# A sigmoid recurrence on one core: the sum in PSUM started by VectorE and finished by TensorE, instead of a product that VectorE adds to

## The chip, the core and the metric

The kernel runs on one core of one Trainium2 chip. The metric is the device time of one execution in microseconds (us); lower is better. TensorE does the matrix products, VectorE and ScalarE the elementwise work on its results in PSUM (eight banks of 512 fp32 columns by 128 partitions), GpSimd works in SBUF only, and SyncE issues most transfers. All data are fp32.

## The reference

A convolutional block with attention and two spectral mixers comes first, and its output is `x` plus a correction. The change lies behind it, in a recurrent layer:

```
Wx = einsum('bti,hi->bth', ln(t), W)   # t: x as 4 batches of 4096 tokens of 128 values
Wx = (Wx - mean) * rsqrt(var + eps) * gamma + beta   # mean and var over all tokens
def step(y, wx_t):
    y = sigmoid(wx_t + y @ V.T)
    return y, y
y0 = 0
_, ys = scan(step, y0, Wx over T)
out = t + ys
```

## The kernel before

The layer's input has 4 batches (`NB`) of 4,096 tokens; each batch is one chain of 4,096 steps of a state with 128 features. The recurrence forgets its start quickly, so the kernel cuts every chain into chunks of `STEPS` = 16 steps and runs all chunks side by side. Every chunk first does `BURN` = 8 steps on the tokens of its own second half from a guessed state, and what that yields is handed to the following chunk as its start; then come the 16 real steps. That makes 24 rounds. A round handles all 1,024 chunks, as four groups `g` = 0..3 (`GR`), one per batch, each a block of 128 features by 256 chunks (`Q` = 8 by `TB` = 32).

In a round a group passes three engines, in one fixed order of instructions on each, and semaphores hand it on:

1. TensorE multiplies the group's last state `y_s` by V into PSUM bank `g` (even rounds of a pair) or `g + 4` (odd ones), 128 x 256 columns: `sums(g, dj)`. It waits for semaphore `state`. Every fp32 product appears in the trace as two weight loads and two MATMUL records. In `from_last`, once in the program (at the first real step, step 0), the state comes from the neighbouring chunk, so it is three products: 1 column of zeros, 31 columns and 224 columns.
2. VectorE adds the scaled input (`add_z`, line 1570): bank = wx_step * bs + bank. It waits for `vy` and signals `vy_wx`.
3. ScalarE takes the sigmoid of the bank into `y_s` (lines 1146 and 1155, unrolled copies of one statement, 256 columns) and signals `state`. In round 0 it needs no product: it reads the scaled input from SBUF with the bias `bb_guess` (line 1142).

So there are 23 rounds with products: seven of four 256-column products, one with `from_last`, and fifteen more of four 256-column products. The body of the loop at the end of `recur` (`e.If(again > 0)`) runs only if the guess was not good enough, which does not happen with these inputs.

Just ahead of the recurrence, 32 products W x are written to SBUF with sums for the normalization (VectorE line 1546, ScalarE line 1133), then a short chain on VectorE (lines 1555 to 1565) makes the scale `bs` and the biases `bb` and `bb_guess`. TensorE there does one product of 1 column for the row sums of V (`v_sum_filled`) and `WARM` = 4 products of 512 columns whose result nobody reads. Behind the recurrence, TensorE transposes the states back (line 636, four transposes for each of 32 results), VectorE adds them to the residual (line 1613), and SyncE stores each result with a transfer of 256 KB. VectorE's check of the guess (lines 1594 to 1604) and the engines' read of the flag come behind that. GpSimd adds `g0` to the residual in 32 pieces (line 620), 21 of them during the recurrence, and then copies the handed-on starts (`start_kept`, line 626), which ScalarE waits for ahead of the last round.

Further ahead, where the second mixer's factors are made, VectorE copies `bet` (line 1513), `z0t` (line 1514) and `g0` (line 1517) out of bank 3; GpSimd waits for `bet`.

The names of lines 632 (products) and 636 (transposes) are those of helpers, `mm` and `tr`; line 400 is the helper `copy`.

Of the kernel before, what the change touches and what calls it, by code (L numbers as in the profile page):

```python
# [67 lines left out]
G0_EARLY, WARM = 11, 4  # L68
# [6 lines left out]
GR = NB  # L75
TOL = 1e-5
# [75 lines left out]
def metaformer(nc, t, out):  # L152
# [4 lines left out]
    with ctx:  # L157
# [289 lines left out]
        def unrolled(n, turn):  # L447

            for i in range(1, n):
                turn(i)  # L450

        def recur(e, sweep, results=None, judge=None):


            def looped(n, turn):
                with e.Fori(1, n) as i:
                    turn(i)


            sweep(0, STEPS - BURN, unrolled)  # L460
            sweep(BURN, 0, unrolled)
            rounds = BURN + STEPS
            if results:
                results(0)
            if judge:
                judge(rounds)
            e.wait_ge(S("judged"), 1)
            again = e.value_load(FLAG[0:1, 0:1], min_val=0, max_val=1)
            with e.If(again > 0):
# [4 lines left out]
                with e.Fori(0, CHUNKS - 1) as i:  # L474
                    sweep(i * STEPS + rounds, 0, looped)
                e.wait_ge(S("state"), GR * (rounds + STEPS * (CHUNKS - 1)))
                if results:
                    results(2)
            e.wait_ge(S("state"), GR * rounds)
# [150 lines left out]
        def _(pe):  # L630
# [228 lines left out]
            def skip_factors(n):  # L859


                if n == 4:
                    pe.wait_ge(S("dg2"), 1)
                    mm(PS[:, 3, 128:256], ones, dg)
# [63 lines left out]
            def sweep(k0, j0, turns):  # L928

                for dj in range(0 if j0 == 0 else 1, 2):  # L930
                    for g in range(GR):
                        pe.wait_ge(S("state"), GR * (k0 + dj - 1) + g + 1)
                        (mm(sums(g, dj), v_t, at(y_s, g, j0)) if dj else from_last(g)).then_inc(S("vy"), 1)

                def turn(i):
                    for dj in range(2):
                        for g in range(GR):
                            pe.wait_ge(S("state"), i * (2 * GR) + (GR * (k0 + dj) + g + 1 - GR))
                            mm(sums(g, dj), v_t, at(y_s, g, i * 2 + (j0 + dj - 1))).then_inc(S("vy"), 1)

                turns((STEPS - j0) // 2, turn)
# [16 lines left out]
            recur(pe, sweep, results, judge)  # L958
# [3 lines left out]
        def _(act):  # L962
# [175 lines left out]
            def sweep(k0, j0, turns):  # L1138
                for dj in range(2):
                    for g in range(GR):  # L1140
                        if j0 and dj == 0:
# [501 lines left out]
```

## Time and profile before

| | |
|---|---|
| time, median of 3 | 427.39 us (427.3 to 428.25) |
| profiled execution | span 424.2 us from first to last instruction; the results list no time of its own for it, so it is set against the median: 3.2 us lie around the span |
| busy share of the span | TensorE 82%, VectorE 80%, ScalarE 54%, GpSimd 50% |
| recurrence | from 346.6 us (first sigmoid) to 390.3 us (first transpose behind it) |
| results and stores | 390.3 us to about 421 us |

The busy shares are averages over stages that have different limits; the recurrence is about a tenth of the span. A MATMUL record is longer than the distance to the next one, since products are pipelined, and VectorE's and ScalarE's instructions overlap by some 0.1 us as well. So what counts is the distance between starts.

### The profile page before, as it was taken

Reading aid. Unit: us, or ns where it says so; the run is one execution under the profiler, and the core shown is the slowest. Engines: PE = TensorE matmul, PEld = TensorE weight load, DVE = VectorE, ACT = ScalarE, POOL = GpSimd, SP = SyncE. Lnnn points to the kernel's source line nnn. Section 1 sums busy time; section 2 is a strip of 40 time slices with the busy share of each in tenths; the row PEclk is TensorE's granted clock in tenths of the full one; section 3 lists DMA queues with packets and bytes.
Section 4 is the critical chain, followed back from the end, with each engine's and each line's share of the span. In section 5 each row is a group of like instructions: output and inputs, shape, how many; then the busy total and the mean of one; then the engine's idle time right before and its main releaser. Section 6 shows DMA issues by size and latency. Waiting matters only on the chain.

```text
span 424.2 us, 7190 instructions
## 1 busy us (share of the span) xinstructions
PE 349.7 (82%) x2415; PEld 273.7 (65%) x2415; DVE 338.0 (80%) x995; ACT 229.5 (54%) x511; POOL 213.0 (50%) x261
## 2 busy tenths in 40 slices
PE   0289979997794899998999778878888789999950
PEld 0289965974352899987988748634454446767950
DVE  2999762766896967469999686999999759899991
ACT  0498851801023388545655125767886789899000
POOL 1389960000002699399892107887886579900000
PEclk9999999999998699999999969899999999999995
DMA  8999998999805000089799880142232500000998
GB/s 215 249 291 319 288 284 191 220 218 379 339 0 199 2 0 2 2 100 116 91 174 119 100 99 2 46 156 100 101 103 107 192 2 0 2 0 0 276 287 234
DMA packets 62999, 59.42 MB, mean 140 GB/s; under 512 B 5792, under 2 KB 55376, under 8 KB 60912
## 3 DMA queue, kind: packets, MB, share of 16 engines
q1 hardware_dynamic: 43232, 50.24, 40.0%
q0 software_dynamic: 16512, 8.39, 16.2%
q10 hardware_dynamic: 3216, 0.30, 0.7%
q8 instruction: 21, 0.34, 0.3%
q14 instruction: 18, 0.15, 0.1%
HBM read 38.84 MB, written 16.94 MB: 131 GB/s over the span
## 4 chain that ended last, share of the span: by engine, by line
DVE 34%; PE 32%; POOL 12%; DMA 6%; issue 5%; SPq 4%; ACT 4%; DVEq 0%; POOLq 0%; ACTq 0%
PE PS L632 30%; POOL BIG L569 8%; DVE SML L1196 6%; DVE BIG L1337 5%; DVE BIG L1529 4%; DVE BIG L1546 3%; SPq L511 3%; DMA BIG<-in_x 3%; DVE BIG L1613 3%; POOL BIG L588 2%; DMA BIG<-BIG 2%; PE PS L636 2%; DMA BIG<-xn_rows 2%; DVE BIG L1429 1%; DVE BIG L1425 1%
## 5 line engine op out<-in xcount | busy, mean ns | idle before, releaser
L632 PE MATMUL PS<-CST,BIG 128*128 128x128 f32 (+6 forms) x994 | 123.0, 312 | 13.1 <-ACT BIG L1004 4.5
L632 PEld LDWEIGHTS PS<-CST,BIG 128*128 128x128 f32 (+1 forms) x994 | 110.2, 193 | 28.8 <-DVE BIG L1529 8.3
L582 POOL COPY BIG<-BIG 128x512 f32<-128x512 f32 x24 | 29.9, 1291 | 79.2 <-DMA BIG<-xn_rows 75.3
L632 PE MATMUL PS<-BIG 128*128 128x128 f32 (+2 forms) x450 | 53.8, 368 | 5.9 <-DVE BIG L1337 5.4
L1196 DVE BATCH_NORM_STATS2 SML<-BIG 128x6 f32<-128x128 f32 x256 | 53.5, 279 | 5.8 <-DMA BIG<-in_x 4.4
L636 PEld LDWEIGHTS PS<-CST,BIG 128*128 128x128 f32 (+1 forms) x326 | 41.6, 183 | 19.5 <-issue 12.4
L632 PEld LDWEIGHTS PS<-BIG 128*128 128x128 f32 (+2 forms) x450 | 40.6, 168 | 16.7 <-issue 8.7
L636 PE MATMUL PS<-CST,BIG 128*128 128x128 f32 (+1 forms) x326 | 49.0, 291 | 2.5 <-ACT SML L400 1.4
L632 PE MATMUL PS<-BIG,SML 128*128 128x256 f32 (+4 forms) x230 | 48.8, 415 | 0.0
L400 ACT ACTIVATE BIG<-PS 128x512 f32<-128x512 f32 (+3 forms) x59 | 32.2, 569 | 26.0 <-PE PS L632 21.0
L569 POOL TENSOR_SCALAR BIG<-BIG,SML 128x128 f32<-128x128 f32 x84 | 40.3, 498 | 9.0 <-DVE SML L1216 9.0
L1570 DVE SCALAR_TENSOR_TENSOR PS<-BIG,SML,PS 128x256 f32<-128x256 f32 x92 | 41.2, 488 | 3.3 <-PE PS L632 3.2
L588 POOL TENSOR_TENSOR BIG<-BIG,SML 128x512 f32<-128x512 f32 x32 | 39.6, 2495 | 7.3 <-ACT BIG L1078 7.3
L632 PE MATMUL PS<-SML 128*128 128x512 f32 (+2 forms) x74 | 35.2, 560 | 9.4 <-DVE BIG L1546 8.0
L611 POOL TENSOR_TENSOR BIG<-BIG 128x512 f32<-128x512 f32 x32 | 40.8, 1275 | 0.5 <-ACT BIG L1104 0.5
L632 PEld LDWEIGHTS PS<-BIG,SML 128*128 128x128 f32 (+1 forms) x230 | 31.0, 178 | 15.2 <-ACT BIG L1155 3.4
L620 POOL TENSOR_TENSOR BIG<-BIG,SML 128x512 f32<-128x512 f32 x32 | 32.0, 1041 | 9.2 <-issue 6.3
L1155 ACT ACTIVATE BIG<-PS,SML 128x256 f32<-128x256 f32 x80 | 35.5, 475 | 0.4
L632 PE MATMUL PS<-SML,BIG 128*128 128x128 f32 (+1 forms) x264 | 33.2, 287 | 1.4 <-DVE SML L1383 1.0
L632 PEld LDWEIGHTS PS<-SML,BIG 128*128 128x128 f32 (+1 forms) x264 | 32.2, 203 | 2.5 <-DVE SML L1383 1.3
L1088 ACT ACTIVATE BIG<-BIG,SML 128x512 f32<-128x512 f32 x32 | 22.8, 720 | 19.0 <-DVE BIG L1425 19.0
L604 POOL TENSOR_TENSOR BIG<-BIG,SML 128x256 f32<-128x256 f32 x32 | 19.6, 613 | 24.4 <-DVE SML L1513 12.5
(218 smaller groups left out, 487.3 us busy)
## 6 DMA issues: line engine op xcount, KB each, us to landing
xn_rows<-BIG SPq DMA_DIRECT2D x8, 1024.0 KB, 9.4
BIG<-xn_rows SPq DMA_DIRECT2D x8, 1024.0 KB, 9.2
BIG<-in_x POOLq DMA_DIRECT2D x8, 1024.0 KB, 11.0
BIG<-rs_rows SPq DMA_DIRECT2D x8, 1024.0 KB, 4.7
out_x<-BIG SPq DMA_DIRECT2D x32, 256.0 KB, 3.6
BIG<-wy_rows SPq DMA_DIRECT2D x16, 192.0 KB, 5.8
BIG<-BIG SPq DMA_DIRECT2D x16, 192.0 KB, 8.0
BIG<-in_L_conv_mixer_w SPq DMA_DIRECT2D x2, 544.0 KB, 9.1
```

What stands on the lines that cost most here:

```text
L400: return e.activation(o, i, ACT.Copy) if e is scalar_engine else e.tensor_copy(o, i)
L569: last = pool.tensor_scalar(x_h[:, n, :], x_h[:, n, :], ln_r[:, n:n + 1], ln_b[:, n:n + 1], ALU.mult, ALU.add)
L582: pool.tensor_copy(x_mix[:, g % MIX_RING], columns(g)).then_inc(S("x_mix_pool"), 1)
L588: pool.tensor_tensor(m1[:, v, :], a0[:, v, :], kap[:, v].unsqueeze(2).to_broadcast([128, 4, W]), ALU.mult).then_inc(S("ka0"), 1)
L611: pool.tensor_tensor(a0[:, v, :], a0[:, v, :], m1[:, v, :], ALU.add).then_inc(S("xm"), 1)
L620: pool.tensor_tensor(a0[:, v, :], a0[:, v, :], g0[:, v].unsqueeze(2).to_broadcast([128, 4, W]), ALU.add).then_inc(S("x1_g0"), 1)
L632: return pe.matmul(o, l, rhs, start=start, stop=stop, **k)
L636: return pe.matmul(o, i, ident[0:n, 0:n], is_transpose=True, start=True, stop=True)
L1088: act.activation(v, v, ACT.Gelu, bias=s("cu")).then_inc(S("m1"), 1)
L1155: act.activation(at(y_s, g, i * 2 + (j0 + dj)), sums(g, dj), ACT.Sigmoid, bias=s("bb")).then_inc(S("state"), 1)
L1196: last = dve.bn_stats(ln_st[:, c % 2, row, :], src[:, XR * c + row, :])
L1570: STT(sums(b, dj), wx_step[:, b, :, bass.ds(j, 1), :], s("bs"), sums(b, dj), ALU.mult, ALU.add).then_inc(S("vy_wx"), 1)
```

## The change

- VectorE no longer adds. Ahead of the product it writes `wx_step * bs` into the bank (`seeded(g, r)`, TENSOR_SCALAR from SBUF to PSUM), up to two rounds ahead, as soon as the sigmoid of round r - 2 has read that bank (semaphore `state`).
- TensorE's product then accumulates on it (`accumulate`, start = False) and waits for both `seed` and `state`; it signals `sum`, for which ScalarE waits directly.
- The product of 1 zero column of `from_last` is gone from the unrolled rounds.
- So that accumulation is defined, eight products of 256 columns write to all eight banks first (semaphore `written`). They take the place of the four of 512 columns and wait for `wx` (VectorE's line 1546) instead of `bn` (ScalarE's line 1133).
- The 1-column product for the row sums of V moves from behind `bn` far ahead, next to the product for `bet`, and VectorE copies its column to SBUF there.
- The loop that isn't run keeps the old way.

```diff
-            pe.wait_ge(S("bn"), G4)
-            mm(PS[:, 7, 511:512], v_t, ones[:, 0:1]).then_inc(S("v_sum_filled"), 1)
-
-            for k in range(WARM):
-                mm(bank(5), v_t, CST[:, 0:512])
+            pe.wait_ge(S("wx"), G4)
+            for k in range(2 * GR):
+                mm(PS[:, k, 0:N_G], v_t, CST[:, 0:N_G]).then_inc(S("written"), 1)
+
+            def accumulate(g, r):
+
+                o, j = seeded(g, r), step_of(r)
+                if j:
+                    return mm(o.rearrange("d (q j t) -> d q j t", q=Q, t=TB), v_t, at(y_s, g, j - 1), False, True,
+                              skip_group_check=True)
+                a, b = TB * g, TB * g + TB
+                last = y_s[:, :, STEPS - 1, a:b]
+                mm(o[:, 1:TB], v_t, last[:, Q - 1, 0:TB - 1], False, True, skip_group_check=True)
+                return mm(o[:, TB:N_G], v_t, last[:, 0:Q - 1, :], False, True, skip_group_check=True)
+
+            def rounds():
+                for r in range(1, ROUNDS):
+                    for g in range(GR):
+                        pe.wait_ge(S("seed"), GR * (r - 1) + g + 1)
+                        pe.wait_ge(S("state"), GR * (r - 1) + g + 1)
+                        accumulate(g, r).then_inc(S("sum"), 1)
```

```diff
+            def rounds():
+                j = step_of(0)
+                for g in range(GR):
+                    act.activation(at(y_s, g, j), wx_step[:, g, :, j:j + 1, :], ACT.Sigmoid,
+                                   scale=s("bs"), bias=s("bb_guess")).then_inc(S("state"), 1)
+                for r in range(1, ROUNDS):
+                    if r == ROUNDS - 1:
+                        act.wait_ge(S("start_kept"), 2 * GR)
+                    for g in range(GR):
+                        act.wait_ge(S("sum"), GR * (r - 1) + g + 1)
+                        act.activation(at(y_s, g, step_of(r)),
+                                       seeded(g, r).rearrange("d (q j t) -> d q j t", q=Q, t=TB),
+                                       ACT.Sigmoid, bias=s("bb")).then_inc(S("state"), 1)
```

```diff
             dve.tensor_copy(bet, PS[:, 3, 128:256]).then_inc(S("bet"), 1)
+            dve.tensor_copy(s("v_sum"), PS[:, 3, 0:1])
             dve.tensor_copy(z0t, PS[0:64, 3, 256:384]).then_inc(S("z0t"), 1)
...
+            def rounds():
+
+                for r in range(1, ROUNDS):
                     for g in range(GR):
-                        dve.wait_ge(S("vy"), GR * (k0 + dj - 1) + g + 1)
-                        add_z(g, dj, j0 + dj)
+                        if r >= 3:
+                            dve.wait_ge(S("state"), GR * (r - 2) + g + 1)
+                        else:
+                            dve.wait_ge(S("written"), GR * (r % 2) + g + 1)
+                        TS(seeded(g, r).rearrange("d (q t) -> d q t", t=TB), wx_step[:, g, :, step_of(r), :],
+                           s("bs"), None, ALU.mult).then_inc(S("seed"), 1)
```

On TensorE, from the last three products W x to the last product of the recurrence, the kernel before has these instructions, with the semaphores that each waits for:

```order
469 L632 MATMUL PS<-SML 128x512 [waits x1,lnw] x3
470 L632 MATMUL PS<-CST,SML 128x1 [waits bn]
471 L632 MATMUL PS<-CST,SML 128x512 x4
472 L632 MATMUL PS<-BIG,SML 128x256 [waits state] x28
473 L632 MATMUL PS<-SML 128x1 [waits state]
474 L632 MATMUL PS<-BIG,SML 128x31
475 L632 MATMUL PS<-BIG,SML 128x224
476 L632 MATMUL PS<-SML 128x1 [waits state]
```

and the changed kernel these:

```order
470 L630 MATMUL PS<-SML 128x512 [waits x1,lnw] x3
471 L630 MATMUL PS<-CST,SML 128x256 [waits wx]
472 L630 MATMUL PS<-CST,SML 128x256 x7
473 L630 MATMUL PS<-BIG,SML 128x256 [waits state,seed] x28
474 L630 MATMUL PS<-BIG,SML 128x31 [waits state,seed]
475 L630 MATMUL PS<-BIG,SML 128x224
476 L630 MATMUL PS<-BIG,SML 128x31 [waits state,seed]
```

The unread products have changed their size and what they wait for, the 1-column products are gone, and each product of the recurrence waits for two semaphores.

On VectorE the end of the normalization's chain and the recurrence read like this before:

```order
531 L1563 TENSOR_TENSOR SML<-SML 128x1 [waits dve_seq]
532 L1565 SCALAR_TENSOR_TENSOR SML<-PS,SML 128x1 [waits v_sum_filled,dve_seq]
533 L1570 SCALAR_TENSOR_TENSOR PS<-BIG,SML,PS 128x256 [waits vy,bn_ab]
534 L1570 SCALAR_TENSOR_TENSOR PS<-BIG,SML,PS 128x256 [waits vy] x91
535 L1613 TENSOR_TENSOR BIG<-BIG,PS 128x512 [waits x1_g0,yt_filled] x32
```

and now:

```order
532 L1581 TENSOR_TENSOR SML<-SML 128x1 [waits dve_seq]
533 L1582 SCALAR_TENSOR_TENSOR SML<-SML 128x1 [waits dve_seq]
534 L1598 TENSOR_SCALAR PS<-BIG,SML 128x256 [waits written,bn_ab]
535 L1598 TENSOR_SCALAR PS<-BIG,SML 128x256 [waits written] x7
536 L1598 TENSOR_SCALAR PS<-BIG,SML 128x256 [waits state] x84
537 L1638 TENSOR_TENSOR BIG<-BIG,PS 128x512 [waits x1_g0,yt_filled] x32
```

The 92 additions that waited for TensorE have become 92 writes that wait for ScalarE of two rounds before.

On VectorE, at the copies out of bank 3, before and then now:

```order
347 L1513 COPY SML<-PS 128x128 [waits z0t_filled]
348 L1514 COPY SML<-PS 64x128
349 L400 COPY BIG<-PS 64x128x4 [waits zt2_filled]
350 L1517 COPY SML<-PS 128x128 [waits g0_filled]
351 L400 COPY BIG<-PS 128x512 [waits ta2_filled]
```

```order
347 L1530 COPY SML<-PS 128x128 [waits z0t_filled]
348 L1531 COPY SML<-PS 128x1
349 L1532 COPY SML<-PS 64x128
350 L402 COPY BIG<-PS 64x128x4 [waits zt2_filled]
351 L1535 COPY SML<-PS 128x128 [waits g0_filled]
```

One copy of a single column stands between those of `bet` and `z0t`.

## Rows read from the trace of the kernel before

**Rows 1.** Chain that ended last, from 330 us: start, length, engine, line.

```profile
343.85 46.63 PE PS L632 x210
```

**Rows 2.** Timeline behind the recurrence: start, length, engine, line, instructions merged.

```profile
390.32 18.82 PE L636 MATMUL PS<-CST,BIG 128*128 128x128 f32 x128
...
391.88 29.17 SPq L538 DMA_DIRECT2D out_x<-BIG  x32
```

**Rows 3.** Timeline of one group's way through a round, 384.4 to 386.4 us.

```profile
384.42 1.60 PEld L632 LDWEIGHTS PS<-BIG,SML 128*128 128x128 f32 x8 [0.19 <-ACT BIG L1155]
...
385.15 0.49 DVE L1570 SCALAR_TENSOR_TENSOR PS<-BIG,SML,PS 128x256 f32<-128x256 f32 x1
...
385.68 0.47 ACT L1155 ACTIVATE BIG<-PS,SML 128x256 f32<-128x256 f32 x1
...
386.20 1.60 PEld L632 LDWEIGHTS PS<-BIG,SML 128*128 128x128 f32 x8 [0.19 <-ACT BIG L1155]
```

**Rows 4.** Timeline at the start of the recurrence, engines PE, PEld, DVE, ACT.

```profile
342.19 0.69 DVE L1546 SCALAR_TENSOR_TENSOR BIG<-PS,BIG 128x512 f32<-128x512 f32 x1 [0.23 <-PE PS L632]
343.85 3.92 PE L632 MATMUL PS<-CST,SML 128*128 128x1 f32 x10 [1.70 <-ACT BIG L1133]
345.32 1.28 ACT L1142 ACT_TABLE_LOAD   x1
346.37 0.16 DVE L1565 SCALAR_TENSOR_TENSOR SML<-PS,SML 128x1 f32<-128x1 f32 x1 [0.29 <-DVE SML L1563]
346.62 2.07 ACT L1142 ACTIVATE BIG<-BIG,SML 128x256 f32<-128x256 f32 x4
347.27 0.19 PEld L632 LDWEIGHTS PS<-BIG,SML 128*128 128x128 f32 x1 [0.33 <-ACT BIG L1142]
347.61 1.49 PEld L632 LDWEIGHTS PS<-BIG,SML 128*128 128x128 f32 x7 [0.16 <-issue]
348.32 1.70 DVE L1570 SCALAR_TENSOR_TENSOR PS<-BIG,SML,PS 128x256 f32<-128x256 f32 x4 [1.79 <-PE PS L632]
348.84 1.26 ACT L1146 ACTIVATE BIG<-PS,SML 128x256 f32<-128x256 f32 x3 [0.15 <-DVE PS L1570]
349.37 0.19 PEld L632 LDWEIGHTS PS<-BIG,SML 128*128 128x128 f32 x1 [0.27 <-ACT BIG L1146]
```

**Rows 5.** Timeline of the weight loads in the round with `from_last`.

```profile
360.10 0.30 PEld L632 LDWEIGHTS PS<-SML 128*128 128x128 f32 x2 [0.20 <-ACT BIG L1155]
...
361.67 0.38 PEld L632 LDWEIGHTS PS<-SML 128*128 128x128 f32 x2
361.97 0.53 PEld L632 LDWEIGHTS PS<-BIG,SML 128*128 128x128 f32 x4
362.49 0.38 PEld L632 LDWEIGHTS PS<-SML 128*128 128x128 f32 x2
```

**Rows 6.** VectorE's groups by shape: count, busy, mean ns of one, idle before.

```profile
L1411 DVE TENSOR_SCALAR BIG<-BIG 128x512 f32<-128x512 f32 x1 | 1.2, 1187 | 0.0
...
L1504 DVE TENSOR_SCALAR BIG<-BIG 128x512 f32<-128x512 f32 x1 | 0.4, 428 | 0.0
```

**Rows 7.** Timeline of GpSimd during the recurrence.

```profile
347.36 20.99 POOL L620 TENSOR_TENSOR BIG<-BIG,SML 128x512 f32<-128x512 f32 x21 [2.92 <-ACT BIG L1142]
```

**Rows 8.** Chain (first two rows) and timeline around the copies out of bank 3.

```profile
256.28 0.20 DVE SML L1513
...
257.27 0.28 DVE SML L1517
...
254.96 0.27 PE L636 MATMUL PS<-CST,BIG 128*64 128x128 f32 x1 [0.39 <-DVE BIG L400]
```

**Rows 9.** Busy time by stretch: PE, PEld, DVE, ACT, POOL, clock, DMA share, GB/s.

```profile
265.20:268.60 3.40, 2.22 (x21) 2.06 (x22) 3.33 (x9) 2.79 (x10) 3.08 (x3) 1.00 0.00 0
268.60:272.00 3.40, 3.40 (x18) 2.67 (x15) 3.26 (x15) 2.97 (x11) 1.80 (x2) 0.51 0.00 0
...
340.50:343.90 3.40, 1.70 (x5) 0.35 (x3) 2.24 (x10) 3.29 (x9) 3.40 (x4) 1.00 0.02 5
```

More of the change, by code:

```diff
@@ L67 @@
 STEPS, BURN = 16, 8
[L68 removed]
+G0_EARLY = 11
 BM_ACT, LEAD, WARM_2 = 2, 6, 3
@@ L75 @@
 GR = NB
+N_G = Q * TB
+ROUNDS = BURN + STEPS
 TOL = 1e-5
@@ L445, in sums, with step_of, seeded, recur @@
             return PS[:, g + GR * dj, 0:Q * TB].rearrange("d (q j t) -> d q j t", q=Q, t=TB)
[L447 to L462, printed above, removed]
+        def step_of(r):
+            return STEPS - BURN + r if r < BURN else r - BURN
+        def seeded(g, r):
+            return PS[:, g + GR * (r % 2), 0:N_G]
+        def recur(e, rounds, sweep, results=None, judge=None):
+            rounds()
             if results:
@@ L465, in recur @@
             if judge:
-                judge(rounds)
+                judge(ROUNDS)
             e.wait_ge(S("judged"), 1)
@@ L926, in from_last, with sweep @@
                 return mm(PS[:, g, TB:Q * TB], v_t, last[:, 0:Q - 1, :])
[L928 to L930 removed]
+            def sweep(k0):
+                for dj in range(2):
                     for g in range(GR):
[L932 to L935 removed]
+                        pe.wait_ge(S("state"), k0 * GR + (GR * (ROUNDS + dj - 1) + g + 1))
+                        (mm(sums(g, dj), v_t, at(y_s, g, 0)) if dj else from_last(g)).then_inc(S("vy"), 1)
+                with pe.Fori(1, STEPS // 2) as i:
                     for dj in range(2):
                         for g in range(GR):
[L938 to L941 removed]
+                            pe.wait_ge(S("state"), i * (2 * GR) + (k0 * GR + (GR * (ROUNDS + dj - 1) + g + 1)))
+                            mm(sums(g, dj), v_t, at(y_s, g, i * 2 + (dj - 1))).then_inc(S("vy"), 1)
             def results(turn):
@@ L956, in judge @@
                 tr(PS[0:1, 0, 0:128], s("gap")).then_inc(S("gap_filled"), 1)
-            recur(pe, sweep, results, judge)
+            recur(pe, rounds, sweep, results, judge)
         @block.scalar
@@ L1149, in turn @@
-                def turn(i):
+                        act.wait_ge(S("vy_wx"), k0 * GR + (GR * dj + g + 1))
+                        act.activation(at(y_s, g, dj), sums(g, dj), ACT.Sigmoid,
+                                       bias=s("bb")).then_inc(S("state"), 1)
+                with act.Fori(1, STEPS // 2) as i:
                     for dj in range(2):
-                        if dj and j0 == 0 and type(i) is int and 2 * i + dj == STEPS - 1:
-                            act.wait_ge(S("start_kept"), 2 * GR)
@@ L1160, in _ @@
-            recur(act, sweep)
+            recur(act, rounds, sweep)
         @block.vector
@@ L1613, in results @@
                     TT(v, v, bank(g % 8), ALU.subtract if turn == 1 else ALU.add).then_inc(S("result"), 1)
-            recur(dve, sweep, results, judge)
+            recur(dve, rounds, sweep, results, judge)
 _NAMES = ["x", "L0_conv_key_w", "L0_conv_key_skip_w", "L0_conv_query_w", "L0_conv_query_skip_w",
```

38 lines of the change are left out of this document (16 added, 22 removed).

## The prediction

> **What bounds the kernel now.** I read the chain that ended last first. Before the stores it runs on TensorE's products without a break from 343.85 us for 46.63 us, through the unread products and the whole recurrence [rows 1]. Behind the recurrence the first transpose starts at 390.32 us, and the stores run from 391.88 us for 29.17 us, all but a few us of what is left of the span [rows 2]. They are issued in a row and start when the first result is there, so what the recurrence gives or takes moves the end by as much.
>
> But "the chain is on TensorE" does not say that TensorE is full. The timeline of one group shows it. Its first weight load begins at 384.42, VectorE's addition at 385.15, ScalarE's sigmoid at 385.68 for 0.47 us, and the load for its next product at 386.20, which had waited for that sigmoid [rows 3]. So a round takes as long as one group's way round: 0.73 (product until addition) + 0.53 (addition until sigmoid) + 0.47 (sigmoid) + 0.05 (until load) = 1.78 us. From 349.37 [rows 4] to 360.10 [rows 5] lie six rounds, which gives it more finely: 10.73 / 6 = 1.788 us. When TensorE never waits, its loads follow each other every (1.49 - 0.19) / 6 = 0.216 us (the row of seven) [rows 4], two to a product of 256 columns: 0.432 us, or 1.73 us for four groups. So the ring of three engines is limited by its latency, yet only 0.06 us a round above TensorE's own rate. That is why removing a stage of 0.53 us from it cannot bring much.
>
> **The recurrence before, taken apart.** The first product streams at 347.61, when the last unread product is through; its load had started at 347.27 [rows 4]. A product streams somewhat behind a load that had waited; I reckon with 0.05 us, an estimate that shifts before and after alike except at the first product. Round 1 lasts until 349.37 + 0.05 = 349.42, that is 1.81. Six rounds of 1.788 make 10.73 and end at 360.15. Fifteen rounds of 1.788 make 26.82 and end at 390.32 [rows 2]; so 363.50 - 360.15 = 3.35 is left for the round with `from_last`, of which one group takes 362.49 - 361.67 = 0.82 [rows 5].
>
> **The change, step by step.**
>
> Addition out of the ring. A group's way round becomes 0.73 + 0.47 + 0.05 = 1.25 us, if ScalarE sees the sum as soon as VectorE did. That is below TensorE's 1.73, so TensorE becomes full and a round costs 1.73. ScalarE can follow: its sigmoids come every (1.26 - 0.47) / 2 = 0.395 us when they are ready [rows 4], against 0.432. So 21 rounds gain 0.060 each: 1.26 us.
>
> VectorE's write. No row shows a TENSOR_SCALAR of 256 columns from SBUF to PSUM. Below stands a TENSOR_SCALAR of 512 columns at 428 ns, above it another of 512 at 1,187 ns [rows 6]; halved for 256 columns these give 0.21 and 0.59 us. The nearest row is the addition that it replaces, with the same SBUF operand, the same scalar and the same output, and one operand more: 0.49 us long, (1.70 - 0.49) / 3 = 0.40 us from start to start [rows 4]. I take 0.40 as the most. It must stay below 0.432 to be hidden. The write for round r needs only the sigmoid of round r - 2, a whole round earlier than the product, so its latency is covered; only its rate could show.
>
> The round with `from_last`. Every small product here costs TensorE a pair of loads that are 0.11 us apart: four loads (31 and 224 columns) begin within 0.53 - 0.19 = 0.34 us [rows 5]. Without the 1-column pair a group takes 0.82 - 0.22 = 0.60, at worst 0.82 - 0.14 = 0.68, if only the streaming of the two shrinks. The round then lasts 2.41 (2.74), and the gain is 3.35 - 2.41 = 0.94 (0.61). I take 0.94, since loads set the pace there.
>
> The start. The eight unread products wait for VectorE's last W x (ends 342.88) instead of ScalarE's last sum (343.85) [rows 4], take 8 x 0.432 = 3.46 us and end at 346.3. So the first product streams at 347.27 + 0.05 = 347.32 instead of 347.61. Its bank is seeded in time: VectorE's chain ends at 346.53 [rows 4], and a write of 0.49 or even 0.59 us is done by 347.15. The four sigmoids of round 0 are done at 346.62 + 2.07 = 348.69 [rows 4], so the fourth group's product is loaded at 348.74, streams at 348.79, and round 2 begins 0.43 later, at 349.22, 0.20 earlier than 349.42. The normalization's chain itself may end 0.2 us earlier, since line 1565 no longer waits for PSUM's column, but that gives nothing: the sigmoid of round 0 starts at 346.62 behind a table load that ends at 346.60 [rows 4].
>
> The moved 1-column product and its copy. On TensorE the product (0.22 us) stands ahead of a stretch in which TensorE idles for 0.39 us waiting for VectorE's copies [rows 8], which hides it; without that cover it would cost 0.22. The copy of one column comes behind `bet`, so GpSimd isn't delayed, but it stands in the chain ahead of `z0t`, `g0` and the first rows of the second mixer. A copy of 128 columns takes 0.20 in that chain [rows 8]; one of a single column takes less. I charge 0.10 (bounds 0 and 0.20).
>
> GpSimd and the end. GpSimd's 21 additions end at 368.35 [rows 7], and ScalarE needs the copies behind them only in the last round, at about 387: they stay hidden. Behind the recurrence nothing changes but that VectorE is free earlier, which the first result doesn't need, as it waits for transposes.
>
> Sum: 1.26 + 0.94 + 0.20 - 0.10 = 2.30 us; by positions, the first transpose starts at 349.22 + 6 x 1.73 + 2.41 + 15 x 1.73 = 388.0 instead of 390.3, and 0.1 later for the copy. The sum is made against the span of 424.2 us, which lies 3.2 below the median; a span of 421.9 and a time of 427.39 - 2.30 = **425.1 us** follow.
>
> **The rivals.**
>
> *The rounds stay as long as they are* (0.18). Only the round with `from_last` and the start gain: 0.94 + 0.20 - 0.10 = 1.04, 426.3 us. For it: the margin is only 0.015 us a product, and each product now waits for two semaphores instead of one, or accumulation onto a bank could stream slightly slower than 0.216. Against it: in a full stretch the load is made one product ahead, so what it waits for may end up to 0.216 - 0.05 = 0.16 us late without harm (with my estimate of 0.05).
>
> *The wait for two semaphores is exposed* (0.05). If it held up each product by 0.05 us, the time from sigmoid to load in rows 3, a product would cost 0.48 and a round 1.93: 21 x 0.14 = 2.9 more, less 1.04: 429.3 us. It decides from 0.015 + 1.04 / 92 = 0.026 us a product on.
>
> *VectorE sets the pace; slower* (0.07). If a write takes as long as the dear row of rows 6 has it, 0.59 us for 256 columns, a round costs 2.37, and the recurrence grows by 21 x 0.58 = 12 us to about 438 us. It decides from about 0.46 us a write on. For it: that row, and that its source is strided like `wx_step`. Against it: the addition with the same strides already manages 0.40.
>
> *GpSimd is slowed so much that ScalarE's last round waits* (within the last case's 0.07, at 0.01). A TENSOR_SCALAR at 428 ns for 512 columns runs faster per column than the addition, so it may use a path into SBUF that GpSimd shares. GpSimd's adds would have to take 1.7 times as long before anything waits (347.36 plus 21 of them plus the copies by 387); at twice they would cost about 5 us, 430 us. By the Trainium skill ("VectorE: DVE Perf Modes", Why PSUM operands drop a tier and Two Vector instructions with no wait between them) a two-port mode reads through an interface shared with GpSimd, but fp32 with a PSUM operand does not get that mode; no run shows it yet.
>
> *TensorE's clock falls in the recurrence* (0.01). The trace has a stretch at the lower level, 1.2 GHz, from 268.6 to 272.0 us, after one in which TensorE was busy for 2.22 of 3.40 us [rows 9]. The change leaves TensorE idle from 346.3 to 347.3. But it idled for 1.70 us before 343.85, and the clock stayed at 2.4 GHz [rows 4, 9]. One such stretch would cost 1.7 us, 426.8 us. The Trainium skill ("TensorE: Matmul & The Clock Gate", What's actually happening) has the clock fall after an idle phase; by that rule the gap here, shorter than the one before, is no danger, and the trace agrees.
>
> *More than forecast* (0.04): products on seeded banks stream faster, or the sum is seen earlier; 424 us or less.
>
> **How the numbers follow.** The forecast has 0.65, with a range of its own from 424.5 to 425.9: the bounds of `from_last` (+0.33), of the copy (-0.10 to +0.10) and of the pace (0.435 instead of 0.432 a product, from the rounding of the row: +0.26), and 0.3 for the scatter of the measurement. The range for 8 in 10 adds the first rival, 424.2 to 426.6. A difference of 0.3% is 1.3 us, about the least that a measurement of this kernel can tell; the line is at 426.1. Faster: 0.65 + 0.04 and a little of the first rival, 0.71. Same: 0.17. Slower: 0.12.
>
> **What would show it.** Right: in the recurrence loads every 0.216 us without waits for ScalarE; rounds of 1.73; sigmoids waiting for TensorE and idle for some 0.05 each; about 2.4 us in the round with `from_last`; VectorE's writes 0.40 or less apart with idle time; the first product at 347.3 + 0.1. Wrong: rounds of 1.79 with waits for `seed`; VectorE without idle time; a first store that isn't 2.3 us earlier; a shift ahead of 340 us of more than 0.2, which I have charged only with the copy and which a different timing of the second mixer's start could bring.

## The result, and the profile after

| | before | after |
|---|---|---|
| median beside each other, 22 runs each | 428.06 us | 426.51 us |
| ratio, with its 95% interval | | 0.9946 (0.9921 to 0.9970) |
| on the 427.39 us of the start | 427.39 us | 425.1 us |
| again, 18 and 12 runs | 427.54 us | 424.67 us, ratio 0.9934 (0.9908 to 0.9960) |
| profiled span | 424.2 us | 420.3 us |
| first sigmoid to first transpose | 43.70 us | 41.39 us |

The changed kernel is faster by 0.5%, 2.3 us (0.9946 is taken over the executions whose clock wasn't held lower than the others', so it isn't the quotient of the two medians; one of the changed kernel's 22 took 611 us at a mean granted clock of 0.56). The two profiles differ by more, 3.9 us, and the table's last line says how much of it belongs to the change: 2.31 us. The rest was there when the first sigmoid began, 1.30 us earlier than in [rows 4], and already at VectorE's copy of `bet`, ahead of which nothing changed but one short product (254.52 us against 256.20, 1.68 earlier); a control run below deals with it.

The chain that ended last, from 330 us to the end (start, length, what), answers to [rows 1]:

```profile
333.89 4.80 DMA BIG<-rs_rows
...
341.61 0.90 ACT BIG L1145 x3
...
344.03 1.28 ACT L1153
345.32 0.61 ACT BIG L1153
346.07 40.81 PE PS L630 x192
386.88 1.16 PE PS L634 x8
```

It now reaches TensorE's products at 346.07, by way of the normalization's chain, the table load of ScalarE and its first sigmoid (both line 1153), and no longer through the unread products. From there to the transposes it is TensorE alone.

The timeline of the tail answers to [rows 2]:

```profile
386.72 18.72 PE L634 MATMUL PS<-CST,BIG 128*128 128x128 f32 x128
...
388.18 29.12 SPq L536 DMA_DIRECT2D out_x<-BIG  x32
```

The transposes start 3.60 us earlier than in [rows 2], the stores 3.70, and the stores take as long as before. So what was gained until 386.7 arrived at the end.

The timeline of all engines in the middle of the recurrence, 380.4 to 382.6 us, answers to [rows 3]:

```profile
380.01 2.63 ACT L1160 ACTIVATE BIG<-PS,SML 128x256 f32<-128x256 f32 x6
380.02 2.75 PE L630 MATMUL PS<-BIG,SML 128*128 128x256 f32 x12
380.08 2.65 DVE L1598 TENSOR_SCALAR PS<-BIG,SML 128x256 f32<-128x256 f32 x6
380.24 2.35 PEld L630 LDWEIGHTS PS<-BIG,SML 128*128 128x128 f32 x11
```

In [rows 3] the loads came in eights, with a wait for ScalarE of 0.19 us between two rows. Here eleven stand in one row without a wait, (2.35 - 0.19) / 10 = 0.216 us apart, the rate of a TensorE that never waits. The sigmoids and the writes run at that pace as well: (2.63 - 0.47) / 5 = 0.432 us.

The start, all engines but GpSimd, answers to [rows 4]:

```profile
341.37 3.72 PE L630 MATMUL PS<-CST,SML 128*128 128x256 f32 x16 [0.83 <-DVE BIG L1564]
...
344.03 1.28 ACT L1153 ACT_TABLE_LOAD   x1
...
344.82 0.16 DVE L1582 SCALAR_TENSOR_TENSOR SML<-SML 128x1 f32<-128x1 f32 x1
345.01 3.20 DVE L1598 TENSOR_SCALAR PS<-BIG,SML 128x256 f32<-128x256 f32 x8
345.32 2.08 ACT L1153 ACTIVATE BIG<-BIG,SML 128x256 f32<-128x256 f32 x4
346.03 0.30 PEld L630 LDWEIGHTS PS<-BIG,SML 128*128 128x128 f32 x2 [1.35 <-DVE PS L1598]
```

The unread products are over at 345.1, the first write starts at 345.01, and the first sigmoid at 345.32 behind the table load that ends at 345.31. The first product is loaded at 346.03, 0.71 us after the first sigmoid starts. The label "<-DVE" is the inference from the last semaphore: the first write, 0.49 us long, had ended at 345.50, and what the load waited for was the first sigmoid (about 0.6 us long, 345.92). Eight writes in 3.20 us are (3.20 - 0.49) / 7 = 0.387 us apart when nothing holds them up.

The weight loads in the round with `from_last` answer to [rows 5], and VectorE's writes as one group with their durations (minimum, median, maximum) to [rows 6]:

```profile
358.41 2.41 PEld L630 LDWEIGHTS PS<-BIG,SML 128*128 128x128 f32 x16
```

```profile
L1598 DVE TENSOR_SCALAR PS<-BIG,SML x92: 475/487/490, 345.0 to 384.0; 128x256 f32<-128x256 f32 x92
```

Sixteen loads in a row, four for each group, 0.60 us a group (2.41 / 4); and no write longer than 0.49 us. GpSimd's additions read as in [rows 7]:

```profile
346.06 20.98 POOL L618 TENSOR_TENSOR BIG<-BIG,SML 128x512 f32<-128x512 f32 x21 [3.24 <-ACT BIG L1153]
```

The waits of the stretch from 345 to 388 us, in full (engine, what it waited for: us in total, times, longest):

```profile
POOL BIG L618 <- ACT BIG L1153: 3.2, 1, 3.2
DVE BIG L1638 <- PE PS L634: 3.0, 1, 3.0
PEld PS L630 <- DVE PS L1598: 1.7, 3, 1.3
PE PS L630 <- ACT BIG L1153: 1.0, 1, 1.0
PEld PS L630 <- issue: 0.2, 1, 0.2
```

In 41 us TensorE waited in the first round alone, where each product still follows its sigmoid of round 0. The copies out of bank 3 (VectorE) answer to [rows 8]:

```profile
254.52 0.27 DVE L1530 COPY SML<-PS 128x128 f32<-128x128 f32 x1
254.71 0.14 DVE L1531 COPY SML<-PS 128x1 f32<-128x1 f32 x1
254.78 0.27 DVE L1532 COPY SML<-PS 64x128 f32<-64x128 f32 x1
...
255.63 0.29 DVE L1535 COPY SML<-PS 128x128 f32<-128x128 f32 x1
```

The one-column copy takes 0.07 us from start to start. And the clock, for which [rows 9] stood, in the stretches ahead of and in the recurrence (busy us of PE, PEld, DVE, ACT, POOL, then PEclk, DMA share, GB/s):

```profile
340.50:343.90 3.40, 2.57 (x13) 2.25 (x13) 1.89 (x12) 2.10 (x7) 2.32 (x3) 1.00 0.01 2
343.90:345.50 1.60, 1.19 (x6) 0.71 (x4) 1.29 (x7) 1.57 (x3) 0.00 (x0) 1.00 0.00 0
...
347.00:388.00 41.00, 41.00 (x199) 36.46 (x198) 37.54 (x89) 39.86 (x93) 21.90 (x29) 1.00 0.00 1
```

TensorE is granted 2.4 GHz throughout.

### The profile page after: what moved, and what is told of

Read it like the earlier page. It is cut to its first block, busy times and chain, and to the rows that moved or that the text cites. A ratio compares the mean times of both kernels' runs of the same rounds, so it can differ in the third digit from the quotient of the medians.

```text
span 420.3 us, 7282 instructions
## 1 busy us (share of the span) xinstructions
PE 347.3 (83%) x2415; PEld 280.8 (67%) x2415; DVE 336.2 (80%) x996; ACT 228.1 (54%) x511; POOL 213.1 (51%) x261
## 4 chain that ended last, share of the span: by engine, by line
PE 35%; DVE 31%; POOL 12%; DMA 8%; issue 5%; SPq 4%; ACT 3%; DVEq 0%; POOLq 0%; ACTq 0%
PE PS L630 33%; POOL BIG L567 8%; DVE SML L1213 6%; DVE BIG L1354 5%; DVE BIG L1547 4%; DVE BIG L1564 4%; SPq L509 3%; DMA BIG<-in_x 3%; DVE BIG L1638 3%; POOL BIG L586 2%; PE PS L634 2%; DMA BIG<-BIG 2%; DMA BIG<-xn_rows 2%; DVE BIG L1446 1%; DVE BIG L1442 1%
## 5 line engine op out<-in xcount | busy, mean ns | idle before, releaser
L630 PE MATMUL PS<-BIG,SML 128*128 128x256 f32 (+4 forms) x230 | 46.8, 409 | 1.0 <-ACT BIG L1153 1.0
L630 PEld LDWEIGHTS PS<-BIG,SML 128*128 128x128 f32 (+1 forms) x230 | 37.5, 179 | 8.7 <-issue 2.5
L630 PE MATMUL PS<-SML 128*128 128x512 f32 (+1 forms) x66 | 34.0, 602 | 9.4 <-DVE BIG L1564 8.0
L609 POOL TENSOR_TENSOR BIG<-BIG 128x512 f32<-128x512 f32 x32 | 40.8, 1276 | 0.6 <-ACT BIG L1116 0.6
L1160 ACT ACTIVATE BIG<-PS,SML 128x256 f32<-128x256 f32 x92 | 39.6, 473 | 0.5
L1598 DVE TENSOR_SCALAR PS<-BIG,SML 128x256 f32<-128x256 f32 x92 | 39.0, 485 | 0.5
```

Source lines behind the costliest of these rows:

```text
L609: pool.tensor_tensor(a0[:, v, :], a0[:, v, :], m1[:, v, :], ALU.add).then_inc(S("xm"), 1)
L630: return pe.matmul(o, l, rhs, start=start, stop=stop, **k)
L1160: act.activation(at(y_s, g, step_of(r)), seeded(g, r).rearrange("d (q j t) -> d q j t", q=Q, t=TB), ACT.Sigmoid, bias=s("bb")).then_inc(S( ...
L1598: TS(seeded(g, r).rearrange("d (q t) -> d q t", t=TB), wx_step[:, g, :, step_of(r), :], s("bs"), None, ALU.mult).then_inc(S("seed"), 1)
```

## The experiments

The measure is the recurrence, from the start of the first sigmoid to the first transpose's MATMUL record; it was 43.70 us before and 41.39 after. It holds all that the change does but the copy at bank 3, and nothing of the scatter ahead of it: from the end of ScalarE's last sum for the normalization to the first sigmoid it is 2.82 or 2.83 us in all twelve profiles, so the chain between them didn't become shorter either. Each value is read from one profile. The times of whole executions scatter too much for these differences: the changed kernel with 240 columns, 2.26 us shorter here, has a ratio of 0.9935 to the kernel before with an interval from 0.9837 to 1.0034. The table gives the measure for all kernels, with the distance of one round from the next (mean over rounds 10 to 21, from the sigmoids):

| kernel | recurrence | round | expected |
|---|---|---|---|
| before | 43.70 | 1.787 | |
| before, again | 43.71 | 1.789 | 43.7 or 45.4 |
| before, without the 1-column products | 42.83 | 1.788 | 42.8, 43.1 or 43.7 |
| before, with the new start | 43.53 | 1.789 | 43.5 or 43.7 |
| before, 240 columns | 44.81 | 1.761 | 43.1 or 41.3 |
| after | 41.39 | 1.727 | 41.3 |
| after, again | 41.39 | 1.727 | 41.4 |
| after, with the 1-column products | 42.28 | 1.727 | 42.3 or 41.9 |
| after, with three more waits a product | 41.39 | 1.727 | 41.4 or 46 to 51 |
| after, 240 columns | 39.13 | 1.620 | 39.0, 40.8 or 41.4 |
| after, a 1-column copy beside each write | 41.52 | 1.728 | 42.6 or 41.4 |
| after, a 64-column copy beside each write | 47.61 | 2.051 | 48.5 |

My theory is the prediction's: before, the latency of the ring of three engines set the pace; after, TensorE's streaming does; the 1-column products cost a pair of loads each. The rivals are that TensorE was the bound before too, that streaming and not loads sets the cost in `from_last`, that the second semaphore costs something, and that VectorE's write is close to the pace.

### The 1-column products, taken away before and put back after

```diff
-                mm(PS[:, g, 0:1], v_t, s("zero"))
```

> The kernel before without the four products of one zero column in from_last, so column 0 of a group's start keeps an old value (the check of the guess is made so lenient that the loop never runs). I measure the recurrence from the start of the first sigmoid to the first MATMUL record of the transposes behind it: 43.70 us before, 41.39 in the changed kernel. If small products cost TensorE a pair of weight loads (my step), the stretch falls by 4 x 0.22 = 0.88 to 42.8 us; if only their streaming counts, by 4 x 0.14 = 0.56 to 43.1. If the ring of three engines, not TensorE, set this round's length, it would stay at 43.7.

```diff
                 last = y_s[:, :, STEPS - 1, a:b]
+                mm(o[:, 0:1], v_t, s("zero"), False, True, skip_group_check=True)
                 mm(o[:, 1:TB], v_t, last[:, Q - 1, 0:TB - 1], False, True, skip_group_check=True)
```

> The changed kernel with the four products of one zero column put back, as accumulating products. Loads theory: the stretch grows by 0.88 to 42.3 us and one group's six loads in that round take 0.82 us again; streaming theory: 41.9 us.

42.83 us and 42.28 us: 0.87 less than before, 0.89 more than after. It is worth the same in either kernel, as an edit on TensorE's own time must be. The weight loads of the second kernel in that round:

```profile
360.10 0.41 PEld L630 LDWEIGHTS PS<-SML 128*128 128x128 f32 x2
360.42 0.53 PEld L630 LDWEIGHTS PS<-BIG,SML 128*128 128x128 f32 x4
360.95 0.38 PEld L630 LDWEIGHTS PS<-SML 128*128 128x128 f32 x2
```

A group goes from 360.10 to 360.95, 0.85 (the three that follow take 0.82 or 0.83), against 0.60 without the pair: the difference of 0.22 is twice the distance of two short loads, 0.11 us, although one column has next to nothing to stream. The rival of streaming (0.56 us for the four) is out. (The first kernel has no 1-column product and so leaves column 0 of each group's first chunk in PSUM as it was. Its whole execution took 433.9 us: the first sigmoid came only at 354.18, behind more low stretches of the clock than in the kernel before, the longest 13.65 us from 179.61.)

### The start alone, in the kernel before

```diff
-            pe.wait_ge(S("bn"), G4)
-            mm(PS[:, 7, 511:512], v_t, ones[:, 0:1]).then_inc(S("v_sum_filled"), 1)
-            for k in range(WARM):
-                mm(bank(5), v_t, CST[:, 0:512])
+            pe.wait_ge(S("wx"), G4)
+            for k in range(2 * GR):
+                mm(PS[:, k, 0:Q * TB], v_t, CST[:, 0:Q * TB])
...
             dve.tensor_copy(bet, PS[:, 3, 128:256]).then_inc(S("bet"), 1)
+            dve.tensor_copy(s("v_sum"), PS[:, 3, 0:1])
```

> The kernel before with the start part of the change alone: eight unread products of 256 columns that wait for wx in place of four of 512 that wait for bn, and the column sums of V moved ahead and copied next to bet. My step: the first product no longer stands behind unread ones, it streams about 0.75 us behind the first sigmoid's start instead of 0.99, and the stretch falls by about 0.2 to 43.5 us. z0t is copied 0.06 to 0.10 us later behind bet than before (0.20 there). Rival: the start gives nothing, since round 1 is paced by the sigmoids of round 0: 43.7.

43.53 us, 0.17 less than before. The copies at bank 3 read as in the changed kernel: `z0t` 0.26 behind `bet` instead of 0.20, `g0` 1.11 instead of 1.05.

This kernel and the changed one with its 1-column products put back differ by the edit at the heart of the change, the addition out of the ring, and the second semaphore that comes with it: 43.53 - 42.28 = 1.25 us. So 43.70 - 41.39 = 2.31 is split into 0.17 + 1.25 + 0.89. That these three add up is no test, since they are the steps of one way from the first kernel to the last; the test is that the 1-column products, measured at both ends of that way, gave 0.87 and 0.89.

### Three more waits ahead of each product, all long satisfied

```diff
                         pe.wait_ge(S("seed"), GR * (r - 1) + g + 1)
+                        pe.wait_ge(S("wt_filled"), 1)
+                        pe.wait_ge(S("kap"), 1)
+                        pe.wait_ge(S("g0"), 1)
                         pe.wait_ge(S("state"), GR * (r - 1) + g + 1)
```

> The changed kernel with three more waits ahead of each of the 92 products on TensorE, for semaphores that were reached long before. If waiting work hides behind the product that streams, up to about 0.16 us a product, nothing changes: 41.4 us, ratio to before 0.995. Rival (the wait for two semaphores is exposed): each instruction that carries waits costs some 0.05 us, one or two more of them a product, 92 x 0.05 to 0.10 = 4.6 to 9.2 us more, 46 to 51 us, ratio 1.005 to 1.016.

41.39 us, no change, and 424.65 us over 10 runs (ratio to before 0.9934, 0.9897 to 0.9972). In the middle of the recurrence the weight loads are again in one row:

```profile
379.89 2.13 PEld L630 LDWEIGHTS PS<-BIG,SML 128*128 128x128 f32 x10
```

(2.13 - 0.19) / 9 = 0.216 us. Five waits a product are as cheap as two, as long as they are satisfied and TensorE is full: they are worked off while the product ahead streams.

Where TensorE stands still until a sigmoid ends, which in the changed kernel it does in the first round alone, there is a difference. The fourth sigmoid of round 0 and the load behind it, with one semaphore (the kernel before with the new start):

```profile
348.47 2.07 ACT L1141 ACTIVATE BIG<-BIG,SML 128x256 f32<-128x256 f32 x4
```

```profile
350.60 0.58 PEld L632 LDWEIGHTS PS<-BIG,SML 128*128 128x128 f32 x3 [0.19 <-ACT BIG L1141]
```

and with two (the changed kernel, whose sigmoids stand above, 345.32 for 2.08):

```profile
347.51 0.54 PEld L630 LDWEIGHTS PS<-BIG,SML 128*128 128x128 f32 x3 [0.20 <-DVE PS L1598]
```

The load comes 0.06 us behind the sigmoid's end in the first and 0.11 in the second (0.05 and 0.11 in unrounded times, and alike for all four groups; 0.11 with five semaphores too). So the rival's 0.05 us for a second semaphore was about right, but it is paid once, in the first round, and not 92 times. No run takes the wait for `seed` alone away, so that it is the second semaphore and not something else in which these products differ is argued, not shown.

### Products of 240 columns, before and after

Both leave the last two of every 32 columns out of the 256-column products, so those get no V y.

```diff
-                        (mm(sums(g, dj), v_t, at(y_s, g, j0)) if dj else from_last(g)).then_inc(S("vy"), 1)
+                        (mm(sums(g, dj)[..., 0:TB - 2], v_t, at(y_s, g, j0)[..., 0:TB - 2]) if dj else from_last(g)).then_inc(S("vy"), 1)
```

> The kernel before with 240 instead of 256 columns in every product of the recurrence but from_last's (two of 32 chunks in each row get no V y; the sigmoids and VectorE's additions keep 256 columns, and the check of the guess is made so lenient that the loop never runs). Theory: before, the ring's latency sets the round. A product is shorter by 2 x 16/256 x 0.216 = 0.027 us and stands in the ring once, so 22 rounds lose 0.027 each: 43.70 - 0.6 = 43.1 us. Rival (TensorE's own pace set the round before too): four products a round, 22 x 4 x 0.027 = 2.4 less: 41.3 us.

```diff
-                    return mm(o.rearrange("d (q j t) -> d q j t", q=Q, t=TB), v_t, at(y_s, g, j - 1), False, True,
+                    return mm(o.rearrange("d (q j t) -> d q j t", q=Q, t=TB)[..., 0:TB - 2], v_t,
+                              at(y_s, g, j - 1)[..., 0:TB - 2], False, True,
```

> The changed kernel with the same cut to 240 columns in every product but from_last's. Theory: TensorE's pace now sets the round, so it falls by 4 x 0.027 in each of 22 rounds: 41.39 - 2.4 = 39.0 us, unless ScalarE (0.395 us from start to start seen before) or VectorE (0.387) holds at 0.405 a product, to which it comes close. Rival (the ring, or VectorE's writes, still sets it): 41.39 - 0.6 = 40.8 or no change.

This is the test of the bound. With a sixteenth fewer columns a TensorE that sets the pace shortens a round by a sixteenth, 0.108 us. After, it does: 1.727 to 1.620, and 41.39 to 39.13 us, where 39.0 was expected. Before, the round went from 1.787 to 1.761, by 0.026: one product's streaming is part of the ring once, not four times.

The stretch of the kernel before came out at 44.81, not 43.1, and the sum of the rounds says that the excess isn't in them: it is in the first one. Its busy times and clock (columns as above):

```profile
342.50:344.50 2.00, 0.22 (x2) 0.22 (x3) 0.95 (x5) 1.73 (x6) 2.00 (x3) 1.00 0.00 0
344.50:348.00 3.50, 3.50 (x6) 1.47 (x6) 1.63 (x11) 2.43 (x4) 0.48 (x2) 0.51 0.01 2
348.00:351.50 3.50, 3.50 (x14) 2.11 (x12) 1.07 (x3) 1.68 (x5) 3.50 (x4) 1.00 0.00 0
```

TensorE was idle for 1.81 us ahead of 344.28, and the clock then fell to 1.2 GHz until 348.0. The unread products, twice as slow, were in the way of the first real one:

```profile
347.05 2.08 ACT L1143 ACTIVATE BIG<-BIG,SML 128x256 f32<-128x256 f32 x4
...
349.74 2.61 PE L632 MATMUL PS<-BIG,SML 128*128 128x240 f32 x11
```

The first real product streams 2.69 us behind the first sigmoid, where it was 347.61 - 346.62 = 0.99 in [rows 4]: 1.70 more. 44.81 - 1.70 = 43.11, which is what the theory has. So the test stands, and it showed a case that the prediction had as a rival for the changed kernel, in the kernel before.

### A second instruction of VectorE beside each write

```diff
+                        dve.tensor_copy(PS[:, g + GR * (r % 2), N_G:N_G + 1], s("bb"))
                         TS(seeded(g, r).rearrange("d (q t) -> d q t", t=TB), wx_step[:, g, :, step_of(r), :],
```

> The changed kernel with a copy of one column into the same bank, which nobody reads, ahead of each of VectorE's 92 writes. A write takes 0.387 us from start to start in the first four; a one-column copy added 0.06 us to its chain elsewhere in the changed kernel. If VectorE's rate is the next limit, 0.387 + 0.06 = 0.447 is above 0.432, and the stretch grows by about 80 x 0.015 = 1.2 us to 42.6, with the products waiting for seed. If the writes have more room than that (cadence shorter when not crowded), it stays at 41.4.

```diff
+                        dve.tensor_copy(PS[:, g + GR * (r % 2), N_G:N_G + 64], wx_step[:, g, 0, 0:2, :])
```

> The same with 64 columns instead of one: 0.06 + 64 columns at about 1.04 ns = 0.13 us more a write, 0.51 us in all, 0.08 above TensorE's 0.432: the stretch grows by about 88 x 0.08 = 7 us to 48.5, TensorE gets waits for VectorE's writes, and the kernel is slower than before. That is the rival in which VectorE sets the pace, made to happen, and shows how far away it was. If it doesn't happen, VectorE's share isn't what I read from the rows.

With one column the recurrence took 41.52 us and the rounds stayed at 1.728. VectorE's timeline at 370 us:

```profile
370.07 0.48 DVE L1599 TENSOR_SCALAR PS<-BIG,SML 128x256 f32<-128x256 f32 x1
370.45 0.15 DVE L1598 COPY PS<-SML 128x1 f32<-128x1 f32 x1
370.51 0.48 DVE L1599 TENSOR_SCALAR PS<-BIG,SML 128x256 f32<-128x256 f32 x1
...
372.75 0.47 DVE L1599 TENSOR_SCALAR PS<-BIG,SML 128x256 f32<-128x256 f32 x1
```

From 370.07 to 372.75 lie six pairs, 0.447 us each. That is slower than TensorE's 0.432, yet TensorE didn't slow down. The reason is that the writes run ahead. From the end of a group's write to the start of its sigmoid there were 1.74 us at the first product, 1.02 at the 25th, 1.52 at the 37th (the round with `from_last` gives VectorE 0.6 us a group to catch up), 0.87 at the 79th and 0.79 from the 85th on, which is the least that a product needs. Only there does TensorE wait:

```profile
384.46 0.30 PEld L630 LDWEIGHTS PS<-BIG,SML 128*128 128x128 f32 x2 [0.15 <-DVE PS L1599]
```

The last products come 0.447 us apart as well, and that is the 0.13 us. The 42.6 on record counted each product's excess of VectorE over TensorE from the start; the lead swallowed nearly all of it, and 41.52 came out close to the 41.4 of a write that stays hidden.

With 64 columns a pair takes (372.74 - 370.18) / 5 = 0.512 us:

```profile
370.18 0.48 DVE L1599 TENSOR_SCALAR PS<-BIG,SML 128x256 f32<-128x256 f32 x1
370.20 0.30 PEld L630 LDWEIGHTS PS<-BIG,SML 128*128 128x128 f32 x2 [0.22 <-DVE PS L1599]
...
372.74 0.48 DVE L1599 TENSOR_SCALAR PS<-BIG,SML 128x256 f32<-128x256 f32 x1
```

From the eighth product on every product waits for VectorE's write but for nine in and behind the round with `from_last`, a round takes 4 x 0.513 = 2.051 us, and the recurrence 47.61 (48.5 was expected; the lead at the start and in `from_last` is what is missing). The whole kernel took 431.5 us in its one run. So the rival "VectorE sets the pace" is a real mechanism, and it sets in as soon as the lead is used up: after 7 products at 0.512 us, after some 83 at 0.447. The change has 0.387 against 0.432.

### Both kernels again, unchanged

> The kernel before once more, as the control for what no edit explains: in the two profiles compared so far the stages ahead of the first changed instruction already differed by 1.7 us. Theory (scatter of transfers and of the clock): the time of the first sigmoid moves by a microsecond or two from one execution to the next with the same code, while the recurrence, from first sigmoid to first transpose, again takes 43.7 us; if TensorE's clock falls in its gap ahead of the unread products, the first round alone is 1.7 us longer, 45.4. Rival (the earlier first sigmoid belongs to the change): the first sigmoid comes at 346.6 again, within 0.3.

> The changed kernel once more, timed with more rounds. Theory: the recurrence takes 41.4 us again and the gain is the 2.3 us of it, a ratio of 0.9946; the first sigmoid lies anywhere from 345.3 to 347.3. Rival (the change also makes the stages ahead of it some 1.3 us shorter): first sigmoid at 345.3 within 0.3 and a gain of 3.6 us, a ratio of 0.9916.

The recurrences repeat within 0.01 us, 43.71 and 41.39. The first sigmoid of the kernel before came at 346.80, within 0.3 of 346.62, so that run by itself came out as the rival had it. What speaks against the rival is the changed kernel, whose first sigmoid moved by 3.05 us with the same code, from 345.32 to 348.37, and so beyond the 347.3 that the theory had allowed as well. Of the kernel before and of the changed one, from ScalarE's timelines:

```profile
346.80 1.59 ACT L1142 ACTIVATE BIG<-BIG,SML 128x256 f32<-128x256 f32 x3
```

```profile
348.37 1.09 ACT L1153 ACTIVATE BIG<-BIG,SML 128x256 f32<-128x256 f32 x2
```

In this pair the changed kernel's is 1.57 later, in the first pair it was 1.30 earlier. So the first pair's 1.30 us is within what the same code scatters by, and the rival as it was put (345.3 within 0.3) is out. A shift of a few tenths ahead of the recurrence isn't: over all profiles the first sigmoid lies from 345.3 to 348.4 with the changed kernel and its variants, and from 346.6 to 348.5 with the kernel before and its variants (354.2 once). The times of whole executions don't decide it either: the second ratio, 0.9934, is 2.8 us, and its interval holds both 0.9946 and the rival's 0.9916. A look at the clock says where it comes from in this pair; of the kernel before and of the changed one:

```profile
255.90:259.30 3.40, 2.63 (x22) 2.20 (x20) 1.80 (x5) 2.10 (x6) 2.51 (x4) 1.00 0.02 5
259.30:262.70 3.40, 3.40 (x34) 3.30 (x34) 2.33 (x7) 1.87 (x6) 3.40 (x4) 1.00 0.00 0
```

```profile
255.90:259.30 3.40, 2.56 (x21) 2.13 (x20) 1.78 (x6) 2.12 (x6) 2.60 (x4) 1.00 0.02 5
259.30:262.70 3.40, 3.40 (x18) 3.21 (x18) 1.31 (x2) 0.87 (x3) 3.40 (x5) 0.50 0.00 0
```

The first rows are alike, and in the second the clock is at half in one kernel, 18 MATMULs instead of 34. I read the time from the copy of `bet` to ScalarE's last sum in all the kernels: 89.1 to 89.3 us in the four with a low stretch from 258 or 259 us (the changed kernel again, with the 1-column products, with the 64-column copy, and the kernel before with the new start), and 87.4 to 87.8 in the others, but for the kernel before without the 1-column products, whose low stretches stand at 265 and 275 us (89.3). So a low stretch there is worth some 1.7 us (1.66 between the two kernels of this pair), and kernels of both kinds had it and were spared.

## Why the prediction was right

*What bounded the kernel before*: right. A round of 1.787 by latency (1.788 in the prediction), shown by the 240 columns, which shorten it by 0.026 and not by 0.108.

*Addition out of the ring*: predicted 1.26, measured 1.25. TensorE is full at 0.216 us a load, 1.727 us a round. That a sum on a seeded bank streams as fast as one on an empty bank was assumed, and the loads show it. The agreement within 0.01 is in part luck: 21 rounds shorter by 0.062 (1.789 to 1.727) are 1.30, and 0.06 of that went into the later loads of the first round.

*VectorE's write*: bounded by 0.21 and 0.59, taken as 0.40 at most; it is 0.487 long and 0.387 from start to start. The row that I held to be nearest, the addition that it replaced, was the right one: dropping the PSUM operand hardly changed its price. At 0.447 us a write the loss was 0.13 us, and at 0.512 it was 6.2. The threshold of 0.46 us, at which the prediction let the gain be used up, left out the lead of two rounds; by a straight line between these two it lies at about 0.47, an estimate.

*The round with `from_last`*: the round after was predicted at 2.41, and 2.41 it is. The length before, taken as a remainder of 3.35, is 3.36 from the first product of that round to the first of the next in the trace (360.14 to 363.50), so by positions the round became 0.95 shorter where 0.94 was predicted. But the 1-column products are not all of it: they account for 0.89 (0.87 in the kernel before), four times the 0.22 of [rows 5]. The other 0.06 comes from how the round begins: in the kernel before its first product had waited for ScalarE. Where TensorE goes into that round without a wait, it takes four groups of 0.825 = 3.30 us with the 1-column products in it; it does so in the changed kernel with them put back, and in the kernel before with the new start. So the prediction had both lengths right and put 0.06 us of their difference down to the wrong cause.

*The start*: predicted 0.20, measured 0.17 in the kernel before. As forecast, the four sigmoids of round 0 and the table load ahead of them limit it; the unread products, over at 345.1, no longer do. In the changed kernel itself less came of it. Round 2 was to begin 2.60 us behind the first sigmoid (349.22 - 346.62) and begins at 2.73: the fourth group's load comes 0.11 behind its sigmoid instead of 0.05, and round 2 begins 0.54 behind that load instead of 0.48. So the first product of `from_last` streams 13.09 us behind the first sigmoid instead of the 12.98 that the prediction's sum gives (13.53 before, as reckoned). This is where the recurrence fell short of the 2.40 us that its three terms make, by 0.09 (the other terms gave 0.02 more by positions).

*The copy*: charged with 0.10 between 0 and 0.20; it puts off the copy of `g0` by 0.06. Whether that reaches the first sigmoid can't be seen, since the stages between vary by more from profile to profile.

*The sum*: 2.31 from the recurrence less 0.06 is 2.25 us, against 2.30 predicted; 425.1 us was predicted, and the ratio on the first median gives 425.1 too. That the two agree within 0.1 is luck: the ratio's interval is 424.0 to 426.1, a repetition gave 0.9934 or 424.6 us, and the terms as the experiments split them were off by 0.01, 0.05 and 0.03 us of gain too much and 0.04 of cost too much.

*The rivals*: that rounds stay as long falls to 1.727; the exposed wait for two semaphores falls to the three extra waits in the full stretch, and shows only in the first round, with 0.06 us; GpSimd's additions take 20.98 us for 21 as before (20.99), so whatever path the write takes into SBUF doesn't slow them. The clock didn't fall in the recurrence in any of the seven profiles of the changed kernel and its variants. I had set it against the changed kernel alone; in one of four profiles of kernels with the old start it fell there and cost 1.70 us. The new start has 0.83 us of idle time ahead of the unread products instead of 1.70. Whether that protects the kernel stays open: one case in four against none in eight with the new start (the kernel before with the new start included) tells nothing certain.

*What would make it wrong*: I had named a shift ahead of 340 us of more than 0.2 as a warning. It came, 1.68 us at bank 3, and would have been taken for gain had I compared the profiles by their spans. It begins with waits for transfers from 91 to 104 us (1.30 us), where both kernels have the same instructions.

## What to carry to other kernels

Where several engines pass work round in a ring, work out both the latency of one trip and the time that the fullest engine needs for all groups: taking a stage out of the ring brings the difference of the two and no more, here 0.06 us of the 0.53 us stage. A product too small to stream anything still costs a pair of loads, 0.22 us here, so splitting off one column in order to clear it is dear next to letting another engine write it. Work that doesn't depend on the ring can be written ahead into a second set of banks; its latency then counts for nothing, and its rate only once the lead is used up, which for a short loop may be never.

## What the runs showed of the hardware that was not expected

Low stretches of TensorE's clock come and go between executions of the same instructions: the changed kernel had one from 259.3 us in one profile and none there in the other, and one from 258 to 259.4 us stood in four of twelve profiles. TensorE's work just ahead of it was the same within 0.1 us of busy time in the two kernels above (2.56 us where the clock fell, 2.63 where it didn't, of 3.4). One costs up to 1.7 us where TensorE is needed and less than can be seen where it isn't: a stretch that began at 267 to 269 us was in four profiles with 87.4 to 87.8 us and missing in three with 87.5 to 87.8. So profiled spans scatter by as much as this change brings, while the stretch between two instructions that enclose the change repeated within 0.01 us.

VectorE's copy of a single column to PSUM is 0.15 us long in its record but adds only 0.06 us to a row of writes (0.447 against 0.387).

Where TensorE stood still for a sigmoid, the load came 0.11 us behind it with two or five semaphores and 0.05 with one, while in a full stretch five waits cost nothing. That the semaphores are the cause of the 0.06 is argued, as said above.
